# Row sums and sums of squares by ones-matmuls in four column tiles and one block transpose

## The reference

```python
q, k, v = (x @ wq.T, x @ wk.T, x @ wv.T)           # per head, 128 wide
q = q * rsqrt(mean(q * q, -1) + 1e-6) * q_norm_w    # k likewise
q, k = apply_rope(q), apply_rope(k)                # position = head here, so a factor per channel
s = 50 * tanh(q @ k.T * scale / 50), causal mask
out = softmax(s) @ v, all heads side by side
x = layernorm(x + out @ wo.T)
x = layernorm(x + moe(x))
```

## Time and profile before

| | |
|---|---|
| time, median of 3 runs | 1281.23 us (1280.22 to 1281.82) |
| profiled execution: span of its instructions | 1275.8 us; 5.4 us less than the median, for what lies around the span |
| TensorE busy | 1137.5 us (89%) |
| VectorE busy | 1077.5 us (84%) |
| GpSimd busy | 745.7 us (58%) |
| ScalarE busy | 700.1 us (55%) |
| mean granted TensorE clock | 0.976 |

### The profile page before, as it was taken

One profiled execution on the slowest core, in us unless ns is written; L12 is line 12 of the kernel. 1 busy time (PEld: TensorE's weight loads), 2 busy tenths in 40 slices (PEclk: granted clock), 3 DMA queues, 4 the chain that ended last, 5 costly groups with the idle time before them and its releaser, 6 DMA issues.

```text
span 1275.8 us, 21790 instructions
## 1 busy us (share of the span) xinstructions
PE 1137.5 (89%) x6879; PEld 963.6 (76%) x6879; DVE 1077.5 (84%) x1683; ACT 700.1 (55%) x1143; POOL 745.7 (58%) x665
## 2 busy tenths in 40 slices
PE   4699999989999999999999999999988878499998
PEld 3578788878888887888888888788877753277788
DVE  5599999999999999999999999999999669814654
ACT  2466666666666666666666666666666523022210
POOL 2366767676666666676667676767677536170001
PEclk9799999999999999999999999999999879799999
DMA  4000100000000000000000011100000070017911
GB/s 149 26 31 25 47 21 29 21 29 21 29 25 25 25 25 25 25 25 25 25 25 25 25 32 33 33 21 29 21 21 17 1 237 1 0 50 199 240 33 54
DMA packets 42142, 55.67 MB, mean 44 GB/s; under 512 B 8864, under 2 KB 34816, under 8 KB 42112
## 3 DMA queue, kind: packets, MB, share of 16 engines
q1 hardware_dynamic: 36336, 49.49, 12.8%
q10 hardware_dynamic: 5200, 4.22, 1.2%
q0 software_dynamic: 576, 1.57, 0.4%
HBM read 49.37 MB, written 4.33 MB: 42 GB/s over the span
## 4 chain that ended last, share of the span: by engine, by line
PE 33%; POOL 26%; DVE 22%; issue 11%; ACT 5%; DMA 2%; POOLq 1%; SPq 0%; DVEq 0%; ACTq 0%
POOL rstd L870 10%; POOL pacc L891 9%; PE ps L358 7%; POOL praw L881 6%; PE ps L360 6%; PE ps L359 6%; DVE qraw L1098 6%; DVE qhat_lo L1015 5%; PE ps L615 3%; PE ps L623 2%; ACT praw L711 2%; DVE qhat_hi L1025 2%; ACT prob_hi L672 2%; PE ps L640 2%; PE ps L641 2%
## 5 line engine op out<-in xcount | busy, mean ns | idle before, releaser
L881 POOL TENSOR_TENSOR praw<-praw,causal 128x128 f32<-128x128 f32 x256 | 211.9, 828 | 236.8 <-ACT praw L711 236.8
L672 ACT ACTIVATE prob_hi<-praw 128x1024 fp32r<-128x1024 f32 (+7 forms) x256 | 171.3, 683 | 216.6 <-POOL praw L881 216.5
L1015 DVE TENSOR_TENSOR prob_lo<-praw,prob_hi 128x1024 fp32r<-128x1024 f32 (+7 forms) x256 | 256.1, 1020 | 38.0 <-ACT prob_hi L672 36.8
L891 POOL TENSOR_TENSOR pacc<-pacc,praw 128x768 f32<-128x768 f32 (+2 forms) x192 | 239.3, 1247 | 28.5 <-POOL praw L881 26.6
L358 PE MATMUL ps<-qhat_hi,kT_hi 128*128 128x512 f32 (+3 forms) x384 | 144.6, 376 | 66.5 <-DVE qhat_lo L1015 42.7
L705 ACT ACTIVATE praw<-ps,rstd 128x1024 f32<-128x1024 f32 (+7 forms) x256 | 182.8, 735 | 11.8 <-PE ps L360 3.0
L711 ACT ACTIVATE praw<-praw 128x1024 f32<-128x1024 f32 (+7 forms) x256 | 163.4, 677 | 0.0
L870 POOL TENSOR_TENSOR rstd<-var,mhalf 128x16 f32<-128x16 f32 x32 | 125.3, 3915 | 60.7 <-DVE var L1053 60.7
L358 PEld LDWEIGHTS ps<-qhat_hi,kT_hi 128*128 128x128 f32 x384 | 73.4, 191 | 93.3 <-issue 40.3
L358 PE MATMUL ps<-prob_hi,vS_hi 128*128 128x512 f32 (+3 forms) x384 | 136.5, 355 | 2.6 <-DVE prob_lo L1015 2.5
L360 PE MATMUL ps<-qhat_hi,kT_lo 128*128 128x512 f32 (+3 forms) x384 | 134.0, 349 | 0.0
(11 more groups left out here) (170 smaller groups left out, 2516.7 us busy)
## 6 DMA issues: line engine op xcount, KB each, us to landing
rqB<-rq_rows SPq DMA_DIRECT2D x32, 512.0 KB, 3.7
wgu<-in_wgu SPq DMA_DIRECT2D x32, 352.0 KB
wd<-in_wd SPq DMA_DIRECT2D x32, 176.0 KB
wraw<-in_wqkv SPq DMA_DIRECT2D x16, 256.0 KB, 3.6
wv<-in_wqkv SPq DMA_DIRECT2D x16, 128.0 KB, 2.1
woraw<-in_wo SPq DMA_DIRECT2D x16, 128.0 KB, 2.0
yacc<-in_x SPq DMA_DIRECT2D x1, 2048.0 KB, 13.9
x_rows<-yacc SPq DMA_DIRECT2D x2, 1024.0 KB, 8.6
```

The source lines that it names most:

```text
L672: return nc.scalar.activation(dst, src, ACT.Copy)
L881: nc.gpsimd.tensor_tensor(diag, diag, causal[:, :], ALU.mult).then_inc(mask_done, 1)
L891: nc.gpsimd.tensor_tensor(pacc[:, b, P * j:T], before, raw, ALU.add).then_inc(pacc_done, 1)
L1015: v.tensor_tensor(dst, x_, hi.bitcast(F32), ALU.subtract).then_inc(done, 1)
```

## The change

It makes both kinds of sum in one way. The squares, and `pacc`, are the moving side of fp32 matmuls, with 128x32 of ones as the stationary side. The 1024 tokens are split into 8 x 4 strips of 32 (j, g, r); strip group g goes to the 32 columns of the array at 32g, by `tile_position`, so four matmuls of 256 moving columns fill 128 partitions of PSUM. All 32 partitions of a group hold the same sums. One VectorE transpose in blocks of 32x32 then brings token 128j + p to partition p, and an instruction with a stride of 32 reads it.

For the squares this takes the place of `fold_squares`, `fold`, `sqp` and the four reads; for `pacc` it takes the place of the eight matmuls, and the unit `sums` now stands as a whole behind the scores of tile 3. The query's `rstd` is now on partition p at place j for token 128j + p, where it was token 8p + j, so the DMA to DRAM writes single elements of 4 bytes. ScalarE waits with the squares until the sums of the step before have been transposed (`squares_free`). `tri`, `onesb` and `iota48`, which only the experts' part reads, move to memory that the attention uses, and GpSimd fills them behind it. The prologue keeps its order.

The diff, cut to its core (left out: the same renumbering of waits elsewhere, arguments that are handed through, and the allocation of the moved constants):

```diff
--- before.py
+++ after.py
@@ -93,7 +93,7 @@
-CONSTS = 23
+CONSTS = 11
@@ -115,15 +115,12 @@
-        ones = sb("ones", [P, 2])
+        ones = sb("ones", [P, 32])
-        tri = sb("tri", [P, P], BF16)
-        onesb = sb("onesb", [P, P], BF16)
-        iota48 = sb("iota48", [P, C], BF16)
@@ -160,13 +157,12 @@
-        fold = asb("fold", [P, P])
-        sqT = asb("sqT", [P, T // 2])
-        sqp = asb("sqp", [P, 2, BLK, TT])
+        sqT = asb("sqT", [P, 2 * 32 * TT])
+        sumT = asb("sumT", [P, 32 * TT])
@@ -310,7 +309,7 @@
             def rq_broadcast(step, b):
                 sp.wait_ge(r_done, step + 1)
-                sp.dma_start(rq_d[b].rearrange("(p j) -> p j", p=P), rstd[:, b, 0:TT]).then_inc(rq_out, 16)
+                sp.dma_start(rq_d[b].rearrange("(j p) -> p j", p=P), rstd[:, b, 0:TT], allow_slow_non_contiguous=True).then_inc(rq_out, 16)
                 sp.wait_ge(rq_out, step * 16 + 16)
                 sp.dma_start(rqB[:, :], rq_d[b:b + 1, :].to_broadcast([P, T])).then_inc(rqB_in, 16)
@@ -386,12 +385,23 @@
                             last = mm(bank[:, P * j:P * j + P], xraw[:, c, t0:t0 + P], wv[:, c, :], start=c == 0, stop=c == KC - 1)
                 last.then_inc(pj_done, 1)
+            def strip_sums(bank_no, c0, by_strip):
+
+                for g in range(BLK):
+                    last = mm(ps[32 * g:32 * g + 32, bank_no, c0:c0 + 32 * TT].rearrange("p (j r) -> p j r", r=32), ones[:, :],
+                              by_strip[:, g], start=True, stop=True, tile_position=(0, 32 * g))
+                return last
+
+            def strips(row):
+                return row.rearrange("p (j g r) -> p g j r", g=BLK, r=32)
+
             def sums_of_squares(step, count, bank_no):
                 open_unit(count)
-                pe.wait_ge(folded, step * 8 + 8)
-                mm(ps[:, bank_no, 0:2 * BLK * TT], fold[:, :], sqp[:, :, :, :].rearrange("p m g j -> p (m g j)"),
-                   start=True, stop=True).then_inc(pj_done, 1)
+                pe.wait_ge(qsq_done, step + 1)
+                strip_sums(bank_no, 0, strips(qsq[:, :]))
+                pe.wait_ge(ksq_done, step * 2 + 2)
+                strip_sums(bank_no, 32 * TT, strips(ksq[:, :])).then_inc(pj_done, 1)
             def scores(s, b, j):
@@ -412,15 +422,11 @@
                                j == 0, (j == 3 and t1 == 512) or j == TT - 1)
                 last.then_inc(pv_done, 1)
-            def sums(s, b, half, count, bank_no):
-
-                if half == 0:
-                    open_unit(count)
-                    pe.wait_ge(pacc_done, (s + 1) * TT + RING)
-                for j in range(TT // 2 * half, TT // 2 * half + TT // 2):
-                    last = mm(ps[:, bank_no, j:j + 1], pacc[:, b, P * j:P * j + P], ones[:, 0:1], start=True, stop=True)
-                if half == 1:
-                    last.then_inc(pj_done, 1)
+            def sums(s, b, count, bank_no):
+
+                open_unit(count)
+                pe.wait_ge(pacc_done, (s + 1) * TT + RING)
+                strip_sums(bank_no, 0, strips(pacc[:, b, :])).then_inc(pj_done, 1)
             def out_proj(s, b, u, count, bank_no):
@@ -468,11 +474,10 @@
                     values(s - 1, 1 - b, 5)
                     values(s - 1, 1 - b, 6)
                     values(s - 1, 1 - b, 7)
-                    sums(s - 1, 1 - b, 0, *hd.unit(b, "sums"))
                 scores(s, b, 2)
                 scores(s, b, 3)
                 if old:
-                    sums(s - 1, 1 - b, 1, *hd.unit(b, "sums"))
+                    sums(s - 1, 1 - b, *hd.unit(b, "sums"))
                     if b == 1:
                         pe.wait_ge(wolo_done, h + 1)
                     out_proj(s - 1, 1 - b, 0, *hd.unit(b, "op0"))
@@ -675,8 +679,14 @@
                 act.wait_ge(xT_in[b], 16 * KC)
                 copy_hi(xT[0][:, :, b * T:b * T + T], xraw[:, :, b * T:b * T + T]).then_inc(xhi_done, 1)
 
-            def projected(what, b, count, bank_no):
+            def squares_free(step):
+
+                if not (isinstance(step, int) and step == 0):
+                    act.wait_ge(folded, step)
+
+            def projected(what, b, step, count, bank_no):
                 if what == "q":
+                    squares_free(step)
                     act.wait_ge(pj_free, count)
                     nc.scalar.activation(qsq[:, :], qraw[:, :], ACT.Square).then_inc(qsq_done, 1)
                     return
...
@@ -931,8 +930,15 @@
             layernorm_rstd(0)
             pool.wait_ge(pj_free, UNITS_ALL)
+            nc.gpsimd.memset(tri[:, :], 1.0).then_inc(pads, 1)
+            nc.gpsimd.memset(onesb[:, :], 1.0).then_inc(pads, 1)
+            nc.gpsimd.iota(iota48[:, :], pattern=[[1, C]], base=0, channel_multiplier=0,
+                           allow_small_or_imprecise_dtypes=True).then_inc(pads, 1)
             for t in (sel, *cum):
                 nc.gpsimd.memset(t[:, 0:PAD, :], 0.0).then_inc(pads, 1)
+            pool.wait_ge(pads, 6)
+            nc.gpsimd.affine_select(out=tri[:, :], in_=tri[:, :], compare_op=ALU.is_gt, fill=0.0, base=0,
+                                    pattern=[[1, P]], channel_multiplier=-1).then_inc(pads, 1)
             nc.gpsimd.memset(grp[:, :, G:G + 5], NEG).then_inc(pads, 1)
             nc.gpsimd.memset(mk[:, :, E:E + 2], NEG).then_inc(pads, 1)
             layernorm_rstd(1)
@@ -1048,12 +1054,10 @@
                 dve.wait_ge(pj_done, count)
                 bank = ps[:, bank_no, :]
                 if what == "ss":
-                    for g in range(BLK):
-                        rows = slice(32 * g, 32 * g + 32)
-                        last = v.tensor_scalar(var[rows, b, :].rearrange("p (m j) -> p m j", m=2),
-                                               bank[rows, 0:2 * BLK * TT].rearrange("p (m g j) -> p m g j", m=2, g=BLK)[:, :, g, :],
-                                               1.0 / DH, RMS_EPS, ALU.mult, ALU.add)
-                    last.then_inc(pj_free, 1)
+                    v.transpose(sqT[:, :], bank).then_inc(folded, 1)
+                    dve.wait_ge(folded, step + 1)
+                    v.tensor_scalar(var[:, b, :], sqT[:, :].rearrange("p (n r) -> p n r", r=32)[:, :, 0],
+                                    1.0 / DH, RMS_EPS, ALU.mult, ALU.add).then_inc(pj_free, 1)
                     return
                 cols = slice(512 * int(what[1]), 512 * int(what[1]) + 512)
                 if what[0] == "q":
@@ -1065,34 +1069,6 @@
                 dst = kT if what[0] == "k" else vS
                 lo_of(dst[1][:, b, cols], bank, dst[0][:, b, cols], pj_free)
-            def fold_squares(step, half):
-                n, cols = half % 2, slice(T // 2 * (half % 2), T // 2 * (half % 2) + T // 2)
-                if half < 2:
-                    dve.wait_ge(qsq_done, step + 1)
-                    src, g, j = qsq[:, cols].rearrange("d (g t j) -> d g j t", t=32, j=TT), BLK // 2, TT
-                    dst = sqp[:, 0, g * n:g * n + g, :]
-                    blocks = sqT[:, :].rearrange("d (g j t) -> d g j t", g=g, j=j)
-                    summed_ = blocks
-                else:
-                    dve.wait_ge(ksq_done, step * 2 + n + 1)
-                    g, j = BLK, TT // 2
-                    src = ksq[:, cols].rearrange("d (j g t) -> d j g t", g=g, t=32)
-                    dst = sqp[:, 1, :, j * n:j * n + j]
-                    blocks = sqT[:, :].rearrange("d (j g t) -> d j g t", j=j, g=g)
-                    summed_ = sqT[:, :].rearrange("d (j g t) -> d g j t", j=j, g=g)
-                count = step * 8 + half * 2
-                if not (isinstance(count, int) and count == 0):
-                    dve.wait_ge(folded, count)
-                v.transpose(blocks, src).then_inc(folded, 1)
-                dve.wait_ge(folded, count + 1)
-                v.tensor_reduce(dst, summed_, AX, ALU.add).then_inc(folded, 1)
             def scale_queries(step, b):
                 dve.wait_ge(rqB_in, step * 16 + 16)
                 v.scalar_tensor_tensor(qraw[:, :], qraw[:, :], gcur[:, :], rqB[:, :], ALU.mult, ALU.mult).then_inc(qf_done, 1)
@@ -1131,7 +1101,9 @@
             def summed(b, count, bank_no):
                 dve.wait_ge(pj_done, count)
-                v.reciprocal(rsum[:, b, :], ps[:, bank_no, 0:TT]).then_inc(pj_free, 1)
+                v.transpose(sumT[:, :], ps[:, bank_no, 0:32 * TT]).then_inc(pj_free, 1)
+                dve.wait_ge(pj_free, count)
+                v.reciprocal(rsum[:, b, :], sumT[:, :].rearrange("p (j r) -> p j r", r=32)[:, :, 0]).then_inc(rsum_done, 1)
             def split_output_weights(hd):
@@ -1158,37 +1130,31 @@
                     tile(s - 1, 4)
                     tile(s - 1, 5)
                     tile(s - 1, 6)
-                if new:
-                    fold_squares(s + 1, 0)
                 if old:
                     tile(s - 1, 7)
                 if new:
-                    fold_squares(s + 1, 1)
```

(2 more changed lines are left out.)

67 lines of the change are left out of this document (25 added, 42 removed).

## The result

The changed kernel takes 1556.24 us (median; 1551.73 to 1557.37), the kernel before, beside it, 1280.72 (1279.32 to 1281.82). The ratio is 1.2138, 95% interval 1.2102 to 1.2174: 275.5 us slower, and far above the upper end of the range, 1372. The profiled execution has a span of 1553.9 us.

The account below looks back on a forecast made before the run. The time of var was taken to set each attention step. Later var and switches gave 1.1 us a step, 31 x 1.1 = +34 us; 1275.8 + 34 + 5.4 = 1315 us, range 1262 to 1372.

Parts of the forecast that it names:

- The row of rq: Write of rstd to DRAM as 1024 4-byte elements: 0.5 to 1.3 us more, hidden before the queries' scaling.
- W: Time from the issue of the row's write to the issue of the broadcast: 1.40 us before, 1.9 to 2.7 forecast.
- The slack: Between the broadcast's landing and its use by the queries' scaling: about 1.4 us more would be hidden.
- the second rival: The row in 4-byte pieces is slow, each microsecond above 2.8 lengthening the step; at 4 us 1352 us; chance 0.14.
- The set of tiles: Four fp32 matmuls on TensorE, each on its own 32 columns, partly overlapped: 1.15 us a set.
- the first rival: All four tiles on TensorE overlap, a set of 0.46 us, 14 us less in all, 1267 us; chance 0.24.
- The switches: TensorE changes between full array and tiles; the three before var together 0 to 0.5 us, taken as 0.2.
- the transposes out of PSUM: New VectorE transposes of 128x512 and 128x256: 0.73 us, with 1.2 as the upper end, and 0.45 for the short one.
- the small instruction: New VectorE read of 128x16 at a stride, before the pow: 0.17 to 0.25 us.
- the fixed stretch behind `var`: From var to the next scores: a fixed 15.7 us, so moving var by x moves the step by x.
- the floor: The pow on GpSimd can't start before pacc of tile 1 is done: at most 1.4 us a step won.
- the third rival: No overlap of the tiles on TensorE, a set of 1.84 us, 99 us more in all, 1380 us; chance 0.17.

Follow-up runs that it names:

- changed_row_undone: The changed kernel with only the DMA of the row written as before, 128 pieces of 32 bytes, so queries get other tokens' factors: 1259.12 us, ratio 0.9833.
- row_contiguous_old_sums: row_contiguous with the eight matmuls of pacc against one column and the old reciprocal, only the squares going by tiles: 1293.12 us, ratio 1.0098.
- row_contiguous: The changed kernel with q strips taken at a stride, so that the row goes to DRAM in runs of 32 bytes again: 1274.97 us, ratio 0.9933.
- squares_first: row_contiguous with the squares' unit moved ahead of the sums, right behind values 7 on TensorE: 1209.63 us, ratio 0.9435.
- squares_first_strided_scale: squares_first with contiguous q strips and the row in 32-byte pieces, VectorE reading rqB at a stride when scaling the queries: 1287.28 us.

## Why the prediction was wrong

**The row of rq: this step failed.** I had W at 1.9 to 2.7 us; it is 10.90 at the median. The slack was right: the broadcast, issued at 597.33 in `changed_row_undone`, lands some 3.7 later and is used at 602.37, so 1.34 us are hidden (I said 1.4). From there every microsecond went into the step, as the second rival said, and in the step read above 11.62 less 1.40 less 1.34 gives 8.88 where VectorE waits 8.86. The mechanism was named, as the second rival, but its price was wrong: I took it from the time of a packet in the DMA's busy share (8.5 to 23 ns, 0.5 to 1.3 us for 56 more to an engine). Packets did behave so, 1024 of them in 1 us. What I priced was not what the wait waits for: nearly 10 us pass behind the last packet. No row of the kernel before held a write of small pieces lying close together, so I had no upper bound, and wrote one all the same.

**The clock behind the wait** was not in the sum at all. A wait of 8 us leaves TensorE idle, and behind it 2.9 to 6.2 us of each step pass at 0.50; 54 to 62 us of the 275. For every rival with a long wait this should have been a term.

**The set of tiles: mis-sized.** I took 1.15 us, with the pairs of one tile in order; it is 0.46. The four tiles run side by side in both of their records, as in the first rival, and `changed_row_undone` at 1259 is near that rival (1267). The switches were sized about right. Into the tiles a switch costs 0.08 us (two matmuls of 512 columns start 0.24 apart, at 718.56 and 718.80, and the set 0.32 behind the second), and as much on the way back (719.58 and 0.46 make 720.04, the next matmul on the full array starts at 720.12); behind `pacc` it is 0.11. The three ahead of `var` make some 0.28 where I took 0.2. The Trainium skill, TensorEngine Tiling (Array Packing), Key Properties, has such a change drain TensorE; the trace agrees, at these 0.08 to 0.11 us a change. The Trainium skill, TensorE: Matmul & The Clock Gate, Part 3, has tiles of different columns run at once; the trace agrees, 0.46 us for eight records whose two would take 0.46 by the earlier trace rows. I had weighed against it its sentence on program order, wrongly: the order holds and the tiles overlap.

**Right:** the transposes out of PSUM (0.72 for 0.73 forecast, 0.45 for 0.45) and the small instruction (0.18); VectorE 5.8 us less a step (23.12 of 29.80 in `changed_row_undone`, 28.90 of 30.54 before), and that this relief by itself is worth little, since the step of `changed_row_undone` is only 0.60 shorter; the fixed stretch behind `var` (`pow` to scores 15.67 before and 15.59 in `changed_row_undone`); and that `var` moves the step one to one. Against the kernel before, scores to `pow` is 0.52 shorter in `changed_row_undone` and the step 0.60; in `row_contiguous_old_sums` against `row_contiguous` both are 0.65 longer. **Half right:** the floor. `pow` does start right behind `pacc` in `squares_first`, but `pacc` was not fixed, nor the 3.95 us of `pow`, and so the step fell by 2.11 and not by at most 1.4.

**The chances.** 0.14 for the second rival at 4 us was a chance for the right mechanism at the wrong price. Its rule with the W of the trace (10.55 on the mean of the steps, less 2.8) gives 31 x 7.75 = 240 us; `pow` to scores is 31 x 7.14 = 221 longer than in `changed_row_undone`, as VectorE's work behind the wait got shorter. The range left out the third rival's 1380, for which I had 0.17, and nothing in it allowed for the clock. An unknown that is followed by an open wait, and with no row near it, asks for a range that is open on that side.

## What to carry to other kernels

A DMA's packets and its completion are two prices: read the second from issue to issue, and ask of every DMA whose layout a change touches how small its pieces are and how close they lie at the target; here 4-byte pieces side by side cost 10 us more than runs of 32 bytes, 64 bytes apart under 2. Where such a write stands in a chain that an engine waits for, price the drop of TensorE's clock behind the wait as well. Where VectorE and GpSimd work side by side, look which instruction starts first: a `prob_lo` 0.4 us behind the `pow` or 0.1 ahead of it made the `pow` 2.9 or 3.9 us long. A change that relieves a busy engine pays when what it frees is used: here all of the change but the row gave 1.7%, and with the squares ahead of the sums the kernel came to 5.6%.

## What the runs showed of the hardware

- 1024 pieces of 4 bytes side by side in DRAM: packets through in about 1 us, SyncE goes on nearly 10 us later; a spread of 9.1 to 12.1 us from issue to issue in one execution.
- Four column tiles of fp32 with 256 moving columns run wholly side by side: 0.46 us for eight records, and 0.08 to 0.11 at each change between tiles and full array. With the moving side at a stride of 8 bytes the set takes 0.48, at 16 or 32 bytes 0.89 and 0.91.
- VectorE instructions with two inputs in SBUF and GpSimd's wait for one another: the scaling of 128x1024 takes 1.28 us with GpSimd idle (740.51 above) and 2.33 where 1.25 of a GpSimd instruction is left at its start; `pow` takes 2.9 us alone and 3.8 to 4.0 where a `prob_lo` has just started.
- In `squares_first_strided_scale`, behind waits of 1.9 us, TensorE's clock was at 0.50 for 3.2 to 3.5 us in 16 steps and at 1.00 in 12; behind the waits of the changed kernel, 6.4 us and more, it was at 0.50 for 2.9 to 6.2 us in all 31.
